# Two attentions in one kernel: how row maxima, row sums and outputs change their layout on the way between partitions and columns

## The chip, the cores and the metric

The program runs on one core of one Trainium2 chip. The metric is the device time of one execution in microseconds (us), the median of several. The core has TensorE (PE, matrix products into PSUM), VectorE (DVE), ScalarE (ACT), GpSimd (POOL, which here works on SBUF tiles alone) and SyncE (SP, which issues DMAs).

## The reference, cut to what matters

Four layers run one after the other on `x` (4 batches, 512 rows, 256 columns), with a context of 1601 rows per batch. Each of the two attentions has 8 heads, so 32 head passes.

```python
x = x + L0_xattn(ctx, layernorm(x))       # stage A: 8 heads of 128, keys: 512 + 1601 rows
x = x + L0_ffn(layernorm(x))              # stage B: top 2 of 8 experts
x = x + L1_xattn(ctx, layernorm(x))       # stage C: 8 heads of 32, keys: 1601 rows
x = x + L1_ffn(layernorm(x))              # stage D: top 2 of 8 experts
# in both attentions, for each batch and head:
attn = softmax(scale * q @ k.T)           # 512 x J, J = 2113 or 1601
out = attn @ v                            # 512 x 128, or 512 x 32
```

## The kernel before

Float32 precision is kept by splitting operands into a high and a low float16 half and making three products (`triple`), or, in stage C, by stacking the halves along the contraction.

**A head is a row of units.** In `attention0` a head `n` has 17 tiles of up to 128 keys, taken in pairs: 9 units, the last with one tile of 65 rows. In `attention1` there are 13 tiles in 7 units. In a unit TensorE makes the scores of its two tiles, transposed (keys on partitions, 512 queries along the columns), into one of two PSUM tiles `psS`; ScalarE takes the exponential twice, as float32 (`pf`) and as float16 (`ph`); VectorE or GpSimd makes the low half (`pl`); and TensorE multiplies both halves with the values into `psO`, some units later (`LAG`: 2 in stage A, 4 in stage C).

**Items.** Between these, at written-out places (`head_items`: unit, place 0 to 3), TensorE works on items, most of them for the next head, each in one of three PSUM tiles `psA` taken in turn. An item may start when the item three before it has been read. Items are: Q, K, V (projections), M (a block of 128 queries by 512 keys of plain scores, from which VectorE takes a row maximum), L (the same for the last few keys), X (the maxima, turned), S (the sums, turned, stage A), O (the output product, stage A), F (the output, turned, stage C), T, N (transposes), W (weights).

**The maximum.** Softmax needs, for each query, a number near the row's maximum. M and L give it with queries on partitions (`mc`, 128 by 4 float32). The scores have queries along columns, so item X turns `mc` into a row of 512 by four float32 transposes at TensorE. In stage A ScalarE then copies the negated row as bfloat16 into row 0 of `mrow` (the other 127 rows are zero), and each score tile gets a fourth product, `oneb` (ones) by `mrow`, that subtracts the maximum. In stage C VectorE writes the negated row as one more row of the stacked queries `qst`, which the score product contracts along with the rest.

**The sum.** In stage A GpSimd adds all 17 tiles of `pf` into `acc` (float32, 128 by 512, line L396). Item S (L613) multiplies `acc` with a column of fours, four float32 products of 128 by 128 with one column, and VectorE takes the reciprocal. In stage C the sum is a column of ones in the values.

**The output.** In stage C `psO` holds 65 rows: 32 of the high half of the values, 32 of the low half, one sum. VectorE copies them to `of` (`out_copy`). Item F multiplies four blocks of `of` with a constant matrix `fold` (65 by 33, float32) that adds the two halves and turns them; VectorE takes a reciprocal and multiplies.

Every engine works through its own list, written out in the same order (`for n`, `for u`, places), and waits on counting semaphores: `s_pG` for GpSimd's low halves, `s_fr` for what VectorE has read, `s_ah` for ScalarE, `s_acc` for the sums.

## Time and profile before

| | |
|---|---|
| time, median of 3 runs | 2724.38 us (2721.0 to 2725.88) |
| the profiled execution: time | 2723.15 us |
| its span | 2721.6 us |
| TensorE busy | 2477.8 us, 91% |
| VectorE busy | 1865.4 us, 69% |
| ScalarE busy | 1675.5 us, 62% |
| GpSimd busy | 1636.6 us, 60% |
| mean granted TensorE clock | 0.958 |

The span is the time from the first to the last instruction. Stage A's loop over heads lies from about 87 to 1505 us, stage B to 1820 us, stage C to 2377 us, stage D to the end. Busy time of TensorE counts a matmul from its start to its modelled end, and matmuls overlap: what one costs a full TensorE is the distance from its start to the next one's start.

### The profile page before, as it was taken

Reading aid. Unit: us, or ns where it says so; the run is one execution under the profiler, and the core shown is the slowest. Engines: PE = TensorE matmul, PEld = TensorE weight load, DVE = VectorE, ACT = ScalarE, POOL = GpSimd, SP = SyncE. Lnnn points to the kernel's source line nnn. Section 1 sums busy time; section 2 is a strip of 40 time slices with the busy share of each in tenths; the row PEclk is TensorE's granted clock in tenths of the full one; section 3 lists DMA queues with packets and bytes.
Section 4 is the critical chain, followed back from the end, with each engine's and each line's share of the span. In section 5 each row is a group of like instructions: output and inputs, shape, how many; then the busy total and the mean of one; then the engine's idle time right before and its main releaser. Section 6 shows DMA issues by size and latency. Waiting matters only on the chain. (4 is left out here: it accounts for less than half of the span.)

```text
span 2721.6 us, 46305 instructions
## 1 busy us (share of the span) xinstructions
PE 2477.8 (91%) x15187; PEld 1489.6 (55%) x15314; DVE 1865.4 (69%) x3467; ACT 1675.5 (62%) x2694; POOL 1636.6 (60%) x1442
## 2 busy tenths in 40 slices
PE   4999999999999999999999389867999999869997
PEld 2455555555555555555554268734555554447886
DVE  5678767787777786777676565347787888677443
ACT  3465665556655566555555375436787878758664
POOL 3467766677667676656567244416676769825443
PEclk9999999999999999999999589979999999969999
DMA  3000000000000000000000383231111101076223
GB/s 117 25 1 1 4 22 1 1 1 1 25 1 1 1 1 1 1 1 1 1 1 0 112 243 78 41 101 40 32 41 26 48 19 30 3 215 188 46 46 66
DMA packets 88377, 107.92 MB, mean 40 GB/s; under 512 B 16322, under 2 KB 77715, under 8 KB 88163
## 3 DMA queue, kind: packets, MB, share of 16 engines
q1 hardware_dynamic: 67140, 76.37, 9.3%
q0 software_dynamic: 19200, 24.97, 5.7%
q10 hardware_dynamic: 1856, 4.19, 0.4%
q8 instruction: 109, 1.79, 0.3%
q14 instruction: 72, 0.59, 0.1%
HBM read 68.75 MB, written 25.88 MB: 35 GB/s over the span
## 5 line engine op out<-in xcount | busy, mean ns | idle before, releaser
L396 POOL TENSOR_TENSOR a_acc<-a_acc,a_pf 128x512 f32<-128x512 f32 (+1 forms) x480 | 645.3, 1344 | 388.0 <-ACT a_pf L524 367.8
L1993 POOL TENSOR_TENSOR c_pl<-c_pf,c_ph 128x512 f16<-128x512 f32 x320 | 378.3, 1210 | 169.0 <-ACT c_ph L2092 168.7
L524 ACT ACTIVATE a_pf<-a_psS 128x1024 f32<-128x1024 f32 (+1 forms) x288 | 281.2, 976 | 303.8 <-PE a_psS L663 300.2
L813 DVE TENSOR_TENSOR a_pl<-a_pf,a_ph 128x512 f16<-128x512 f32 x448 | 405.4, 914 | 28.2 <-ACT a_ph L530 28.2
L789 DVE TENSOR_REDUCE a_mx<-a_psA 128x1 f32<-128x512 f32 x512 | 344.9, 685 | 48.8 <-PE a_psA L600 42.6
L530 ACT ACTIVATE a_ph<-a_psS 128x1024 f16<-128x1024 f32 (+1 forms) x288 | 281.0, 976 | 0.0
L1303 POOL DMA_INDIRECT f_sums<-f_xn,f_sidx x78 | 138.9, 1781 | 228.1 <-DVE f_xn L1668 191.6
L2324 DVE TENSOR_REDUCE c_mx<-c_psA 128x1 f32<-128x512 f32 x384 | 251.0, 685 | 34.4 <-PE c_psA L2163 32.4
L2085 ACT ACTIVATE c_pf<-c_psS 128x1024 f32<-128x1024 f32 x192 | 197.7, 1030 | 89.4 <-PE c_psS L2197 88.5
L784 DVE TENSOR_TENSOR a_vl<-a_psA,a_vh 128x256 f16<-128x256 f32 (+1 forms) x272 | 115.2, 423 | 167.2 <-ACT a_vh L469 164.3
L1162 DVE TENSOR_TENSOR f_xn<-f_xn 128x256 f16<-128x256 f32 x312 | 129.6, 424 | 127.8 <-ACT f_xn L1133 123.5
L685 PE MATMUL a_psO<-a_pl,a_vh 128*128 128x512 f16 (+1 forms) x544 | 206.8, 380 | 5.4 <-POOL a_pl L401 5.4
L679 PE MATMUL a_psO<-a_ph,a_vh 128*128 128x512 f16 (+1 forms) x544 | 207.1, 381 | 1.0 <-DVE a_ol L818 1.0
L542 PE MATMUL a_psS<-a_qh,a_kh 128*128 128x512 f16 (+1 forms) x544 | 206.2, 379 | 0.9 <-ACT a_mrow L485 0.8
L680 PE MATMUL a_psO<-a_ph,a_vl 128*128 128x512 f16 (+1 forms) x544 | 206.8, 380 | 0.0
L544 PE MATMUL a_psS<-a_qh,a_kl 128*128 128x512 f16 (+1 forms) x544 | 206.7, 380 | 0.0
L543 PE MATMUL a_psS<-a_ql,a_kh 128*128 128x512 f16 (+1 forms) x544 | 206.5, 380 | 0.0
L600 PE MATMUL a_psA<-a_kh,a_qh 128*128 128x512 f16 x512 | 194.3, 380 | 4.6 <-DVE a_kl L778 1.2
L778 DVE SCALAR_TENSOR_TENSOR a_kl<-a_psA,a_bkv,a_kh 128x512 f16<-128x512 f32 (+1 forms) x160 | 105.4, 659 | 134.3 <-ACT a_kh L463 134.3
L2092 ACT ACTIVATE c_ph<-c_psS 128x1024 f16<-128x1024 f32 x192 | 197.4, 1028 | 0.0
L1062 PE MATMUL f_psH<-f_xh,f_w 128*128 128x256 f16 x624 | 173.1, 277 | 17.7 <-ACT f_xn L1133 9.0
L463 ACT ACTIVATE a_kh<-a_psA,a_bkv 128x512 f16<-128x512 f32 (+1 forms) x160 | 98.3, 614 | 123.8 <-PE a_psA L544 123.8
(329 smaller groups left out, 6382.8 us busy)
## 6 DMA issues: line engine op xcount, KB each, us to landing
f_stage<-in_L_ffn_w SPq DMA_DIRECT2D x16, 1024.0 KB, 5.6
f_stage<-in_L_ffn_W SPq DMA_DIRECT2D x16, 1024.0 KB, 5.3
c_kst<-c_khs SPq DMA_DIRECT2D x64, 100.1 KB, 2.2
a_cx<-in_ctx SPq DMA_DIRECT2D x4, 1536.0 KB
c_cx<-in_ctx SPq DMA_DIRECT2D x12, 512.0 KB, 4.1
f_xrow<-f_xn SPq DMA_DIRECT2D x8, 512.0 KB, 3.2
f_sums<-X SPq DMA_DIRECT2D x2, 2048.0 KB, 12.4
c_kst<-c_kls SPq DMA_DIRECT2D x32, 100.1 KB, 2.2
```

The source lines that it names most:

```text
L396: g.tensor_tensor(acc[0:k, p, :], acc[0:k, p, :], pf[0:k, q % RF, i, :], ALU.add).then_inc(s_acc, 1)
L524: act.activation(pf[0:r, q % RF, 0:k, :], psS[q % 2][0:r, 0:k, :], ACT.Exp, scale=SCALE).then_inc(s_pF, 1)
L530: act.activation(ph[0:r, q % RP, 0:k, :], psS[q % 2][0:r, 0:k, :], ACT.Exp, scale=SCALE).then_inc(s_pH, 1)
L543: pe.matmul(out, hi, xl_, start=False, stop=False)
L544: return pe.matmul(out, lo, xh_, start=False, stop=last)
L679: pe.matmul(psO[:, :], vh[0:r, g % 2, j, vs], ph[0:r, q % RP, i, :], start=(j == 0), stop=False)
L680: pe.matmul(psO[:, :], vl[0:r, g % 2, j, vs], ph[0:r, q % RP, i, :], start=False, stop=False)
L685: ins = pe.matmul(psO[:, :], vh[0:r, g % 2, j, vs], pl[0:r, q % RP, i, :], start=False, stop=(j == JT0 - 1))
L789: v.tensor_reduce(mx[:, n % 2, it, c:c + 1], ps[:, 0:KCH[c][1]], AX.X, ALU.max).then_inc(s_fr, 1)
L813: v.tensor_tensor(pl[0:r, q % RP, i, :], pf[0:r, q % RF, i, :], ph[0:r, q % RP, i, :], ALU.subtract).then_inc(s_pL, 1)
L1993: g.tensor_tensor(pl[0:r, q % RP, i, :], pf[0:r, q % RF, i, :], ph[0:r, q % RP, i, :], ALU.subtract).then_inc(s_pG, 1)
L2324: ins = v.tensor_reduce(mx[:, n % 2, it, c:c + 1], ps[:, 0:KCH[c][1]], AX.X, ALU.max)
```

## The change

1. **Stage A, maxima.** Item X and ScalarE's copy go. GpSimd multiplies a negated identity with the maxima, broadcast (`row`): `mrow` then holds, in each block of 128 columns, a diagonal matrix with the negated maxima, and the product with ones sums its columns. `row(n + 1)` stands in the last but one unit (`TOP`), ahead of that unit's sums. TensorE waits for it ahead of the fourth product of a head's first score tile.
2. **Stage A, sums.** ScalarE copies `acc` to float16 (`sum_hi`, at the head of unit 1 of the next head), GpSimd makes the low half (`sum_lo`, at the head of unit 2), and item S makes eight float16 products.
3. **Stage C, maxima.** `mc` is float16, and item X multiplies with a float16 identity.
4. **Stage C, outputs.** Item F is four plain transposes of `of` (65 rows), without `fold`; VectorE adds the two halves in PSUM, with one instruction more.

```diff
@@ stage A
-                               (6, 3, ("L", m)), (7, 2, ("X", m))):
+                               (6, 3, ("L", m))):
...
+            def sum_lo(n):
+                g.wait_ge(s_sh, n + 1)
+                if n >= 1:
+                    g.wait_ge(s_it, IDX[("S", n - 1)] + 1)
+                g.tensor_tensor(sl[:, :], acc[:, n % 2, :], sh[:, :], ALU.subtract).then_inc(s_sl, 1)
+
+            def row(n):
+
+                g.wait_ge(s_mc, n + 1)
+                g.tensor_tensor(mrow[:, n % 2, :].rearrange("p (t q) -> p t q", q=P),
+                                minus[:, :].unsqueeze(1).broadcast_to([P, ST, P]),
+                                mc[:, n % 2, :].unsqueeze(2).broadcast_to([P, ST, P]), ALU.mult).then_inc(s_mrow, 1)
...
+                    if n >= 1 and u == SUM_AT:
+                        sum_lo(n - 1)
+                    if u == TOP and n + 1 < NH:
+                        row(n + 1)
                     sums(n, u)
...
-                elif what[0] == "X":
-                    act.wait_ge(s_it, i + 1)
-                    act.activation(mrow[0:1, what[1] % 2, :], ps[0:1, :], ACT.Copy, scale=-1.0).then_inc(s_ah, 1)
...
+            def sum_hi(n):
+                act.wait_ge(s_acc, added(uid(n, U - 1)))
+                if n >= 1:
+                    act.wait_ge(s_it, IDX[("S", n - 1)] + 1)
+                act.activation(sh[:, :], acc[:, n % 2, :], ACT.Copy).then_inc(s_sh, 1)
...
+                    if n >= 1 and u == SUM_AT - 1:
+                        sum_hi(n - 1)
...
-                    pe.wait_ge(s_acc, added(uid(n, U - 1)))
+                    pe.wait_ge(s_sl, n + 1)
                     for it in range(ST):
-                        ins = pe.matmul(ps[:, it:it + 1], acc[:, n % 2, it * P:(it + 1) * P], four[:, :], start=True,
-                                        stop=True)
-                elif what[0] == "X":
-                    n = what[1]
-                    pe.wait_ge(s_mc, n + 1)
-                    for it in range(ST):
-                        ins = pe.transpose(ps[0:1, it * P:(it + 1) * P], mc[:, n % 2, it:it + 1], identf[:, :])
+                        for part in (sh, sl):
+                            ins = pe.matmul(ps[:, it:it + 1], part[:, it * P:(it + 1) * P], four[:, :],
+                                            start=part is sh, stop=part is sl)
...
-                        pe.wait_ge(s_ah, after_act(("X", n)))
                 ps = psS[q % 2][0:r, i, :]
                 triple(ps, kh[:, p, js], kl[:, p, js], qh[:, p, :], ql[:, p, :], True, False)
+                if u == 0 and i == 0:
+                    pe.wait_ge(s_mrow, n + 1)
@@ stage C
-                        ins = pe.transpose(ps[0:1, it * P:(it + 1) * P], mc[:, n % 2, it:it + 1], identf[:, :])
+                        ins = pe.matmul(ps[0:1, it * P:(it + 1) * P], mc[:, n % 2, it:it + 1], ident[:, :], start=True,
+                                        stop=True)
...
-                        ins = pe.matmul(ps[:, it * (DH + 1):(it + 1) * (DH + 1)], of[:, it * P:(it + 1) * P],
-                                        fold[:, :], start=True, stop=True)
+                        ins = pe.transpose(ps[:, it * VC:(it + 1) * VC], of[:, it * P:(it + 1) * P], identf[0:VC, 0:VC])
...
+                    v.reciprocal(rl[:, n % 2, :], pt[:, :, 2 * DH]).then_inc(s_rl, 1)
+                    v.tensor_reduce(both, pt[:, :, 0:2 * DH].rearrange("p t (a n) -> p t n a", a=2), AX.X, ALU.add).then_inc(s_rl, 1)
+                    v.wait_ge(s_rl, 2 * n + 2)
```

The change moves work between engines at three places. GpSimd, stage A, from a head's last low half for unit 4 to the next head's unit 2. Before (`a_pl` is a low half, `a_acc` the sum, `X` the output rows):

```order
L401 TENSOR_TENSOR a_pl<-a_pf,a_ph 128x512
L396 TENSOR_TENSOR a_acc<-a_acc,a_pf 128x512 x2
L362 TENSOR_TENSOR X<-X,a_yt 128x256 x2
L401 TENSOR_TENSOR a_pl<-a_pf,a_ph 128x512
L396 TENSOR_TENSOR a_acc<-a_acc,a_pf 128x512 x2
```

Now:

```order
L421 TENSOR_TENSOR a_pl<-a_pf,a_ph 128x512
L414 TENSOR_TENSOR a_mrow<-a_minus,a_mc 128x512
L403 TENSOR_TENSOR a_acc<-a_acc,a_pf 128x512 x2
L403 TENSOR_TENSOR a_acc<-a_acc,a_pf 65x512
L398 TENSOR_TENSOR a_acc<-a_pf 128x512
L403 TENSOR_TENSOR a_acc<-a_acc,a_pf 128x512 x2
L409 TENSOR_TENSOR a_sl<-a_acc,a_sh 128x512
L403 TENSOR_TENSOR a_acc<-a_acc,a_pf 128x512 x6
```

Two instructions of 512 columns are new per head: the diagonal right behind the head's last low half (that of unit 6), the low half of the sum behind the next head's unit 1.

TensorE, stage C, around item F, before:

```order
L2163 MATMUL c_psA<-c_kst,c_qst 128x512
L2180 MATMUL c_psA<-c_fold,c_of 128x33 x4
L2221 MATMUL c_psO<-c_ph,c_vst 65x512
L2226 MATMUL c_psO<-c_pl,c_vst 65x512
L2197 MATMUL c_psS<-c_qst,c_kst 128x512
L2169 MATMUL c_psA<-c_kst,c_qst 128x65 x4
```

Now:

```order
L2188 MATMUL c_psA<-c_kst,c_qst 128x512
L2206 MATMUL c_psA<-identf,c_of 128x65 x4
L2246 MATMUL c_psO<-c_ph,c_vst 65x512
L2251 MATMUL c_psO<-c_pl,c_vst 65x512
L2222 MATMUL c_psS<-c_qst,c_kst 128x512
L2194 MATMUL c_psA<-c_kst,c_qst 128x65 x4
L2222 MATMUL c_psS<-c_qst,c_kst 128x512
L2246 MATMUL c_psO<-c_ph,c_vst 65x512
L2251 MATMUL c_psO<-c_pl,c_vst 65x512
L2246 MATMUL c_psO<-c_ph,c_vst 65x512
L2251 MATMUL c_psO<-c_pl,c_vst 65x512
L2200 MATMUL c_psA<-c_ident,c_mc 1x128 x4
```

The order is as it was; F (L2180, now L2206) gives 65 columns instead of 33, and X (now L2200) takes another identity.

VectorE, stage C, the same place, now:

```order
L2349 TENSOR_REDUCE c_mx<-c_psA 128x1 x2
L2362 RECIPROCAL c_rl<-c_psA 128x4
L2363 TENSOR_REDUCE c_psA<-c_psA 128x128
L2367 TENSOR_TENSOR c_yt<-c_psA,c_rl 128x128
L2352 TENSOR_REDUCE c_mx<-c_psA 128x4
L2306 TENSOR_REDUCE c_mc<-c_mx 128x4
L2378 TENSOR_TENSOR c_pl<-c_pf,c_ph 128x512
L2356 TENSOR_SCALAR c_qst<-c_psA 1x512
```

One row is new, L2363, the sum of the two halves. It stands between item F and the maxima that item X turns.

## Rows read from the trace of the kernel before

**Rows 1.** The page: span, busy times, granted clock in 40 slices

```profile
span 2721.6 us, 46305 instructions
PE 2477.8 (91%) x15187; PEld 1489.6 (55%) x15314; DVE 1865.4 (69%) x3467; ACT 1675.5 (62%) x2694; POOL 1636.6 (60%) x1442
PEclk9999999999999999999999589979999999969999
```

**Rows 2.** Windows of stages A and C: length, busy PE PEld DVE ACT POOL, clock, DMA

```profile
87.00:1505.00 1418.00, 1399.72 (x7806) 758.83 (x7930) 1027.04 (x1700) 847.95 (x1265) 963.43 (x792) 1.00 0.01 3
1820.00:2377.00 557.00, 511.69 (x2660) 272.00 (x2660) 436.51 (x751) 419.38 (x488) 396.54 (x358) 0.95 0.13 32
```

**Rows 3.** Waits of TensorE in stage A: us, times, longest

```profile
PE a_psO L685 <- POOL a_pl L401: 5.4, 6, 2.0
```

**Rows 4.** Timeline of TensorE, stage A: start, us, line

```profile
612.42 0.29 PE L607 MATMUL a_psA<-a_kh,a_qh 128*128 128x65 f16 x4
612.54 0.38 PE L542 MATMUL a_psS<-a_qh,a_kh 128*128 128x512 f16 x1
822.24 0.38 PE L600 MATMUL a_psA<-a_kh,a_qh 128*128 128x512 f16 x1
822.45 0.95 PE L613 MATMUL a_psA<-a_four,a_acc 128*128 128x1 f32 x8
823.26 0.38 PE L679 MATMUL a_psO<-a_ph,a_vh 128*128 128x512 f16 x1
842.40 0.60 PE L619 MATMUL a_psA<-identf,a_mc 128*1 128x128 f32 x4
842.84 0.38 PE L679 MATMUL a_psO<-a_ph,a_vh 128*128 128x512 f16 x1
```

**Rows 5.** Timeline of GpSimd, stage A, a usual head and one with more work

```profile
841.98 1.15 POOL L401 TENSOR_TENSOR a_pl<-a_pf,a_ph 128x512 f16<-128x512 f32 x1
843.09 4.61 POOL L396 TENSOR_TENSOR a_acc<-a_acc,a_pf 128x512 f32<-128x512 f32 x3
258.51 1.15 POOL L401 TENSOR_TENSOR a_pl<-a_pf,a_ph 128x512 f16<-128x512 f32 x1
```

**Rows 6.** Timeline of TensorE and ScalarE at the same two places

```profile
844.78 0.38 PE L685 MATMUL a_psO<-a_pl,a_vh 128*128 128x512 f16 x1
259.81 0.38 PE L685 MATMUL a_psO<-a_pl,a_vh 128*128 128x512 f16 x1 [0.40 <-POOL a_pl L401]
848.46 0.38 PE L663 MATMUL a_psS<-a_mrow,a_oneb 128*128 128x512 bf16 x1
854.28 0.69 ACT L463 ACTIVATE a_kh<-a_psA,a_bkv 128x512 f16<-128x512 f32 x1 [2.23 <-PE a_psA L544]
```

**Rows 7.** Timeline of TensorE, stage C, one head and a chunk's transposes

```profile
2068.14 0.28 PE L2122 MATMUL c_psA<-identf,c_cx 65*128 65x65 f32 x2
2310.22 0.38 PE L2221 MATMUL c_psO<-c_ph,c_vst 128*65 128x512 f16 x1 [0.81 <-DVE c_of L2357]
2310.87 0.98 PE L2180 MATMUL c_psA<-c_fold,c_of 65*128 65x33 f32 x8
2311.68 0.38 PE L2221 MATMUL c_psO<-c_ph,c_vst 128*65 128x512 f16 x1
2313.54 0.60 PE L2175 MATMUL c_psA<-identf,c_mc 128*1 128x128 f32 x4
2313.98 0.38 PE L2197 MATMUL c_psS<-c_qst,c_kst 97*65 97x512 f16 x1
```

**Rows 8.** Timeline of VectorE, stage C, in the same head

```profile
2311.07 0.69 DVE L2324 TENSOR_REDUCE c_mx<-c_psA 128x1 f32<-128x512 f32 x1 [0.40 <-PE c_psA L2163]
2311.88 0.18 DVE L2335 RECIPROCAL c_rl<-c_psA 128x4 f32<-128x4 f32 x1
2312.66 0.43 DVE L2327 TENSOR_REDUCE c_mx<-c_psA 128x4 f32<-128x260 f32 x1 [0.27 <-PE c_psA L2169]
2313.12 0.17 DVE L2281 TENSOR_REDUCE c_mc<-c_mx 128x4 f32<-128x16 f32 x1
```

More of the change, by code:

```diff
@@ L95, in attention0 @@
     TOP = U - 2
+    SUM_AT = 2
     ON_POOL = {(4, 1), (5, 1), (6, 1)}
@@ L150, in opening @@
         out.insert(out.index(("M", 0, 0, 0)), ("B", 0))
-        return out + [("L", 0), ("B", 1), ("V", 0, v), ("X", 0)]
+        return out + [("L", 0), ("B", 1), ("V", 0, v)]
     OPEN = opening()
@@ L261, in attention0 @@
         oneb = sb("oneb", [P, P], BF16)
+        minus = sb("minus", [P, P], BF16)
         onef = sb("onef", [P, P], F32)
-        four = sb("four", [P, 1], F32)
+        four = sb("four", [P, 1], F16)
         zcol = sb("zcol", [P, 1], F32)
@@ L299, in attention0 @@
         s_mc = sem("mc")
+        s_mrow = sem("mrow")
         s_sP = sem("sP")
@@ L306, in attention0 @@
         s_acc = sem("acc")
+        s_sh = sem("sh")
+        s_sl = sem("sl")
         s_oH = sem("oH")
@@ L343, in _ @@
         def _(g):
-            for t, v in ((mhalf, -0.5), (onef, 1.0), (four, 4.0), (mv, 0.0), (oneb, 1.0), (mrow, 0.0), (zcol, 0.0)):
+            for t, v in ((mhalf, -0.5), (onef, 1.0), (four, 4.0), (mv, 0.0), (oneb, 1.0), (zcol, 0.0)):
                 g.memset(t[:], v).then_inc(s_const, 1)
+            g.tensor_scalar(minus[:, :], identf[:, :], -1.0, None, ALU.mult).then_inc(s_const, 1)
             g.wait_ge(s_const, 7)
@@ L407, in _ @@
                 item(what)
+            row(0)
             g.wait_ge(s_fr, after_dve(("B", 1)))
@@ L425, in _ @@
                             item(what)
+            sum_lo(NH - 1)
             for what in CLOSE:
@@ L533, in _ @@
                         item(what)
+            sum_hi(NH - 1)
             out_hi(NH - 1)
@@ L1871, in attention1 @@
         cth, ctl = sb("cth", [P, 2, KC, 512], F16), sb("ctl", [P, 2, KC, 512], F16)
-        mx, mc = sb("mx", [P, 2, ST, NK]), sb("mc", [P, 2, ST])
+        mx, mc = sb("mx", [P, 2, ST, NK]), sb("mc", [P, 2, ST], F16)
+        ident = sb("ident", [P, P], F16)
         pf = sb("pf", [P, RF, 2, S])
@@ L1916, in attention1 @@
         names = ("L1_xattn_Wq", "L1_xattn_Wk", "L1_xattn_Wv")
-        NCONST = 7
+        NCONST = 5
         @block.sync
@@ L1973, in rstds @@
                 g.tensor_scalar(ve[:, :], mv[:, :, 1], EPS, None, ALU.add).then_inc(s_pool, 1)
-                g.wait_ge(s_pool, b + 1 if b == 0 else 2 + b + 1)
+                g.wait_ge(s_pool, b + 1 if b == 0 else b + 2)
                 g.tensor_tensor(rstd[:, :], ve[:, :], mhalf[:, :], ALU.pow).then_inc(s_rstd, 1)
-            for i, (t, val) in enumerate(((mhalf[:, :], -0.5), (ones, 1.0), (fold[:, :], 0.0), (fold[2 * DH:VC, DH:DH + 1], 1.0),
+            for i, (t, val) in enumerate(((mhalf[:, :], -0.5), (ones, 1.0),
                                           (vst[:, :, :, :, 2 * DH:VC], WS), (vf[:, :, :, DH:2 * DH], 0.0),
@@ L1982, in _ @@
             rstds(0)
-            g.wait_ge(s_rstd, 1)
-            for i in range(2):
-                g.affine_select(out=fold[0:2 * DH, 0:DH], in_=fold[0:2 * DH, 0:DH], compare_op=ALU.not_equal, fill=1.0,
-                                base=-i * DH, pattern=[[-1, DH]], channel_multiplier=1).then_inc(s_pool, 1)
-                g.wait_ge(s_pool, i + 2)
+            g.tensor_copy(ident[:, :], identf[:, :]).then_inc(s_pool, 1)
             def low(q, i):
@@ L2233, in _ @@
             pe.wait_ge(s_const, NCONST)
-            pe.wait_ge(s_pool, 3)
+            pe.wait_ge(s_pool, 2)
             for what in FIRST:
@@ L2333, in item @@
                     n = what[1]
-                    pt = ps[:, 0:ST * (DH + 1)].rearrange("p (t n) -> p t n", n=DH + 1)
-                    v.reciprocal(rl[:, n % 2, :], pt[:, :, DH]).then_inc(s_rl, 1)
-                    v.wait_ge(s_rl, n + 1)
+                    pt = ps[:, 0:ST * VC].rearrange("p (t n) -> p t n", n=VC)
+                    both = ps[:, ST * VC:ST * VC + ST * DH].rearrange("p (t n) -> p t n", n=DH)
+                    v.reciprocal(rl[:, n % 2, :], pt[:, :, 2 * DH]).then_inc(s_rl, 1)
+                    v.tensor_reduce(both, pt[:, :, 0:2 * DH].rearrange("p t (a n) -> p t n a", a=2), AX.X, ALU.add).then_inc(s_rl, 1)
+                    v.wait_ge(s_rl, 2 * n + 2)
                     if n >= 2:
                         v.wait_ge(s_x, n - 1)
-                    ins = v.tensor_tensor(yt[:, n % 2, :, :], pt[:, :, 0:DH],
+                    ins = v.tensor_tensor(yt[:, n % 2, :, :], both,
                                           rl[:, n % 2, :].unsqueeze(2).broadcast_to([P, ST, DH]), ALU.mult)
```

10 lines of the change are left out of this document (5 added, 5 removed).

## The prediction

> **What bounds the kernel now.** I read the windows of the two stages first, then who TensorE waits for, then the timeline at the places that the change touches. The page gives the span of the profiled execution, 2721.6 us, with TensorE busy for 91% of it and at full clock in nearly all of stage A [rows 1]. In stage A TensorE is busy 1399.7 of 1418 us [rows 2]: it is the bound, and what shortens its list shortens the stage, as long as no other engine takes over. The others stand at 60 to 72% there; GpSimd, which gets work from the change, at 963 of 1418 us. Its low halves already make TensorE wait, but only 5.4 us in 6 waits [rows 3]. In stage C TensorE is busy 511.7 of 557 us, the others 71 to 78% [rows 2]; here the slack is less clear, and I follow one head.
>
> What a matmul costs a full TensorE is the distance from start to start, not its duration: 512 float16 columns take 0.21 to 0.22 us (822.24 to 822.45), though the row says 0.38 [rows 4].
>
> **Stage A, the sums (S).** Four float32 products of 128 by 128 with one column are eight records, and they hold TensorE from 822.45 to 823.26, 0.81 us, 0.10 each [rows 4]. They become eight float16 products with one column. The nearest row is item L: four products of 65 float16 columns, each with its own 128 by 128 weights, in 0.12 us (612.42 to 612.54), 0.03 each [rows 4]. A shorter one can't cost more than that unless its weight load is the limit, and these four had such loads. I take 8 x 0.03 = 0.24 us, so 0.57 saved per head. Bounds: 0.2 for the eight below, 0.81 (no gain) above.
>
> A rule of the Trainium skill speaks against this. TensorE: Matmul & The Clock Gate, section LDWEIGHTS, has a weight load take columns / 1.2 ns, which is 107 ns for 128 columns whatever the type, an estimate of 0.85 us for eight and so nothing gained. The trace's float32 records at 0.10 us agree with it, its float16 ones at 0.03 don't, and the sum goes by these.
>
> **Stage A, the maxima (X).** Four float32 transposes hold TensorE from 842.40 to 842.84, 0.44 us [rows 4]. They go, and the product with `mrow` keeps its shape, so its 0.22 us stay. 0.44 saved per head, and ScalarE's copy with it, whose place `sum_hi` takes.
>
> **Who hides the new work.** GpSimd gets two instructions of 512 columns per head. Its low halves of that size take 1.15 us, its sums up to 4.61 / 3 = 1.5 [rows 5]; I take 1.2 each, 1.5 as the upper bound for the one with two broadcast inputs, which no row shows. That is 77 us more, 1040 of a stage of some 1390: 75%. What counts is where they stand.
> - The diagonal stands behind the head's last low half, which ends at 841.98 + 1.15 = 843.13, so it is done at 844.4. TensorE needs it for the first product with `mrow` of the next head, at 848.46 [rows 5, 6]. 4 us of slack.
> - The last low half itself is needed at 844.78 [rows 6], 1.65 us after it is done. GpSimd's run that leads to it starts with an exponential of unit 4, behind S but ahead of X. So the gain at S moves both, and the gain at X comes out of the 1.65 us: it fits, in a usual head. In the three heads that also add the output bias, TensorE waits 0.40 for it already (259.81) [rows 6]; there X's 0.44 turn into wait. The other three of the six waits lie in the last two heads, whose TensorE has less to do; there too I count nothing.
> - In those three heads the low half ends at 258.51 + 1.15 = 259.66 [rows 5] and the diagonal at 260.9 (261.2 at 1.5). TensorE wants it seven products after 259.81, at 261.3. It just fits.
> - The sum of the head is complete at 843.09 + 4.61 = 847.70 now and at 848.9 then [rows 5]. ScalarE's copy of it stands ahead of the K item at 854.28, before which ScalarE was idle for 2.23 us, from 852.05 [rows 6]. Behind the copy are queued that K item and the exponential of unit 1, for which TensorE's next scores wait; 3.2 us of slack hide it. The low half (1.2) comes behind the sums of unit 1, and S reads it in unit 3. Without that cover each would cost its full wait.
>
> At the end of the stage nothing hides the copy and the low half of the last sum: some 0.6 + 1.2 us between the sum and S in place of none, in part beside the last output's own path, and the last head is short for GpSimd. I take +1.5. At the opening, TensorE no longer stops for a turned row ahead of the first scores: -0.7, from the 0.44 and a copy, against the 1.2 of GpSimd that three products hide in part. Stage A: -(30 x 0.57) - (27 x 0.44) + 1.5 - 0.7 = -28.2 us.
>
> **Stage C.** X: four products of 128 float16 columns lie between the 0.03 of 65 and the 0.22 of 512 [rows 4], so 0.055 each, 0.22 in place of 0.44 (2313.54 to 2313.98) [rows 7]: 0.22 saved. F: eight records from 2310.87 to 2311.68, 0.81 us [rows 7], become four transposes of 65 columns. Two such, float32 from 65 rows, last 0.28 together, of which one alone is about 0.2 (0.29 less three steps of 0.03 in L's row [rows 4]): a step of at most 0.08. Half of a 128-column transpose's 0.11 is 0.055. I take 0.25 for four, 0.56 saved; the upper bound is the 0.10 of the float32 records now, 0.41 for four and 0.40 saved. Together 0.78 per head.
>
> But VectorE pays. The new sum of halves reads 256 elements from PSUM, and a reduction of 260 takes 0.43 us [rows 8]. It stands between F and the maxima that X waits for. Followed through: F would be done at 2311.12, but VectorE is in the reduction that began at 2311.07, so its reciprocal begins at about 2311.7 (now 2311.88). With 0.1, 0.43 and some 0.25 for the product the reduction of L starts at 2312.5 (now 2312.66, where it waits for TensorE), the maxima are there 0.6 later, as now, at 2313.15 [rows 8], and X starts at 2313.2. TensorE would be ready for it at 2313.54 - 0.56 = 2312.98. So X waits 0.2 us, and F's 0.56 shrink to 0.34. With X's 0.22 the head gains 0.56.
>
> The wait for `of` stays: TensorE stands 0.81 us at 2310.22 in each such head [rows 7], for a copy that follows a reduction that follows TensorE's own product. All that moves together. Heads with items for the next batch have more of TensorE's work between F and X, and may gain the full 0.78; I take 0.56 for all, and 31 heads, since the first one of the stage ends in a wait for a load. Stage C: -17.4 us.
>
> **Sum.** -28.2 - 17.4 = -45.6. The profiled execution took 2723.15 us, so 2677.6; the median of the runs lay 1.2 above it, hence 2678.
>
> **The rivals.** (a) VectorE takes more of stage C: if the sum of halves costs 0.6 to 0.8 us, for its strided input or for the wait for two results, F's gain is gone, and stage C gives 31 x 0.22 = 7 us. For it speaks VectorE's 78% and the single reduction's worth of room; against it, that the row of 260 elements is of the same kind. 2688.
> (b) S costs what it did, by the weight loads: 30 x 0.57 come back, 2695. Against it are the four loads in 0.12 us.
> (c) GpSimd takes over in the late units of stage A: TensorE's 5.4 us of waits grow by X's gain, 12 us; 2690. For it speaks that it works without a break there (841.98 to 847.70), against it the 1.65 us.
> (d) Slower than before: ScalarE, a strict list, stands before the copy of the sum and holds the exponentials behind it. That begins once GpSimd completes the sum more than 3.2 us later than now, and costs 32 us for each further us; from 3.2 + 45.6 / 32 = 4.6 us on the kernel is slower than before. It would take a diagonal product of over 4 us, three times what any row of that size takes. At 5.5 us later: 2678 + 32 x 2.3 = 2752.
>
> **How the numbers follow.** Forecast 0.74 (its own range 2664 to 2688: below, the full 0.78 in stage C and 0.2 us for S, 57 us in all; above, F at its upper bound and the diagonal late in some heads), (a) 0.10, (b) 0.05, (c) 0.06, (d) 0.04, no effect at all 0.01. Range 2662 to 2694, which leaves out (d), most of (b) and the edges. Faster means by over 0.2%, below 2719, about what a measurement of this kernel tells from no change: 0.94. Same 0.02, slower 0.04.
>
> **What the profile after would show.** S in about 0.24 us (wrong: near 0.8, that is (b)); no X and no new wait of a score product for GpSimd in stage A; heads shorter by 1.0 us there; at most 0.9 us of wait for a low half in the bias heads; F in 0.25 us; a wait of X for the maxima of about 0.2 us in heads without items for the next batch, and those heads 0.56 us shorter. Wrong would make it: a sum of halves well above 0.43 us, ScalarE waiting for GpSimd's sum in each head, or a diagonal product of several us.

## The result and the profile after

The changed kernel took 2696.76 us (median of 4 runs, 2693.58 to 2698.33), the kernel before 2724.02 us (median of 4 on the same chip, 2721.0 to 2725.88). The ratio is 0.9899, with a 95% interval of 0.9882 to 0.9917: faster by some 27 us. The prediction had 2678 and a range up to 2694. The sign and most of the steps were right; 19 us of the forecast gain of 46 are missing, and the time is outside the range.

The page of the kernel after; its rows answer to [rows 1]:

```profile
span 2695.6 us, 46041 instructions
PE 2436.9 (90%) x15057; PEld 1425.6 (53%) x15058; DVE 1903.7 (71%) x3499; ACT 1675.4 (62%) x2694; POOL 1734.4 (64%) x1503
```

The windows of stages A and C after, with the columns of [rows 2]:

```profile
85.00:1492.00 1407.00, 1377.47 (x7807) 724.70 (x7806) 1056.25 (x1700) 850.42 (x1266) 1059.67 (x858) 0.99 0.01 3
1800.00:2349.00 549.00, 495.11 (x2550) 243.12 (x2550) 445.40 (x786) 420.83 (x490) 399.74 (x357) 0.95 0.13 34
```

TensorE's busy time fell by 22 us in stage A and by 17 in stage C. But stage A's window is only 11 us shorter: of the 22 us taken out, some half came back as idle time. VectorE runs the same 1700 instructions there as before and is busy for 29 us *more* (1056 against 1027). An engine whose work has not grown and whose busy time has is being slowed, and this is the line to follow up.

The waits of TensorE in stage A after, with the columns of [rows 3]:

```profile
PE a_psO L714 <- POOL a_pl L421: 15.6, 7, 3.2
PE a_psA L574 <- DVE a_kl L807: 5.0, 7, 0.9
PE a_psO L708 <- DVE a_ol L847: 3.9, 4, 1.8
```

GpSimd's low half makes TensorE wait 15.6 us instead of 5.4, and the longest of these waits is 3.2 us. Of the waits in the two last rows there was one each before (0.9 us for `a_kl`, 1.0 for `a_ol`); now there are 7 and 4.

To place the time I measured from one head's reciprocal of the sums to the next one's (of `a_rl` in stage A, of `c_rl` in stage C), in both traces. The first of them comes 2.3 us earlier, the 31 heads that follow in stage A take 10.9 us less, those of stage C 15.7 us less, and what lies between the stages and behind stage C takes 1.4 us more each time. The sum is 26.0, the difference of the spans. Head by head in stage A, where head n is what ends with the n-th reciprocal after the first (us, from the trace):

| heads | before | after | forecast |
|---|---|---|---|
| 4 to 7, 12 to 15, 20 to 29 | e.g. 43.73 | 42.73 | -1.01 |
| 8, 16 | 43.73 | 43.82 | -1.01 |
| 1, 9, 17 | 44.39 | 43.64 | -1.01 |
| 2, 10, 18 | 45.00 | 44.54 | -1.01 |
| 3, 11 (with the bias) | 45.81 | 49.44 | -0.57 |
| 19 (with the bias) | 45.80 | 47.75 | -0.57 |

Eighteen heads did what was forecast, to 0.01 us. Three gave back 10.9 us against the forecast, eight more 4.6. The last two, which the forecast had 1.5 us longer for the end of the stage, became 1.6 longer together, and the opening with its one head gained 2.3 for a forecast of 1.7.

**Head 3.** GpSimd's timeline in the kernel after (start, us, line):

```profile
252.27 2.77 POOL L369 TENSOR_TENSOR X<-X,a_bb 128x256 f32<-128x256 f32 x4
255.00 3.54 POOL L421 TENSOR_TENSOR a_pl<-a_pf,a_ph 128x512 f16<-128x512 f32 x1
258.50 1.08 POOL L414 TENSOR_TENSOR a_mrow<-a_minus,a_mc 128x512 bf16<-128x512 bf16 x1
```

VectorE's timeline at the same place, after:

```profile
254.96 1.05 DVE L782 TENSOR_SCALAR a_cx<-a_cx,a_mv,a_rstd 128x256 f32<-128x256 f32 x3
255.92 1.28 DVE L842 TENSOR_TENSOR a_pl<-a_pf,a_ph 128x512 f16<-128x512 f32 x2
257.13 1.56 DVE L782 TENSOR_SCALAR a_cx<-a_cx,a_mv,a_rstd 128x256 f32<-128x256 f32 x2
```

And VectorE's there in the kernel before, where GpSimd's low half began at 258.51 and took 1.15 [rows 5]:

```profile
258.90 2.18 DVE L753 TENSOR_SCALAR a_cx<-a_cx,a_mv,a_rstd 128x256 f32<-128x256 f32 x2
```

Both engines read and write SBUF here, and the rows look as if one of them stood still while the other works. Before, GpSimd began 0.39 us ahead of VectorE; its low half took 1.15 and VectorE's two norms 2.18, where three alone take 1.05. After, VectorE began 0.04 us ahead; four norms (0.40 each) and two low halves (0.68 each) ran at full speed one behind the other, and GpSimd's low half took 3.54. It ended at 258.54; less its own 1.15, it got nowhere until about 257.4, when VectorE had a last norm to make, of 65 rows. That one took 1.24. TensorE and its clock behind it, after (a timeline, then a window of five us, whose last three values are clock, DMA share and GB/s):

```profile
258.69 0.40 PE L714 MATMUL a_psO<-a_pl,a_vh 128*128 128x512 f16 x1 [3.23 <-POOL a_pl L421]
259.31 0.63 PE L709 MATMUL a_psO<-a_ph,a_vl 128*128 128x512 f16 x1
259.00:264.00 5.00, 5.00 (x17) 1.90 (x16) 1.13 (x1) 0.40 (x1) 4.78 (x4) 0.67 0.01 2
```

TensorE waits 3.23 us where it waited 0.40 [rows 6], and just after the standstill it starts eight products at the lower of its two clock levels, 1.2 GHz: they stand 0.43 apart, not 0.22, some 1.7 us more. 2.83 + 1.7 is 4.5 of the 4.6 us that the head is above the trend of its neighbours. In head 19 the wait is the same 3.23 and the clock stays up; it lost 3.0.

The Trainium skill, SBUF — State Buffer, section Who interferes with whom, says that VectorE and GpSimd share a pair of ports, that the instruction which starts first has it to the end, and that the other one blocks fully. It says so for VectorE instructions with two inputs in SBUF, as the low halves have, and for those in a mode that uses two ports, which a `tensor_scalar` such as the norms can enter; no run here shows in which mode the norms ran. On who waits for whom, these two traces agree with it. The page speaks of one instruction; here the low half of 1.15 us stayed out over four norms and two low halves, 2.4 us, and why it was let in only then no run shows.

**The new waits for VectorE.** TensorE in head 8, after, at the first product of the V item, and VectorE ahead of it:

```profile
503.85 0.28 PE L574 MATMUL a_psA<-a_wkvh,a_xth 128*128 128x256 f16 x1 [0.66 <-DVE a_kl L807]
501.83 1.29 DVE L842 TENSOR_TENSOR a_pl<-a_pf,a_ph 128x512 f16<-128x512 f32 x1
503.05 0.74 DVE L807 SCALAR_TENSOR_TENSOR a_kl<-a_psA,a_bkv,a_kh 128x512 f16<-128x512 f32 x1
```

V's product takes the PSUM buffer that `a_kl` still reads. It used to come 0.57 us later, behind the long float32 S. And the low half ahead of `a_kl` takes 1.29 us beside GpSimd, where it takes 0.68 alone and took 0.68 before. V stands 0.82 us later for it; with the M item at 498.92, which starts 0.26 late behind `a_vl`, that is what head 8 lies above the forecast. The 448 low halves of VectorE in stage A are busy for 440.9 us after and for 405.4 before. Of these 35 us not all are the change's: in `stage_c_only` below, whose stage A is that of the kernel before, they are busy for 419.7, with every head but the last as long as before. VectorE's busy time pointed to the right place, but what it costs has to be read from TensorE's waits.

**Stage C.** TensorE in a head without items for the next batch, after (F at L2206, X at L2200):

```profile
2285.22 0.41 PE L2206 MATMUL c_psA<-identf,c_of 65*128 65x65 f32 x4
2285.46 0.38 PE L2246 MATMUL c_psO<-c_ph,c_vst 128*65 128x512 f16 x1
...
2287.10 0.38 PE L2251 MATMUL c_psO<-c_pl,c_vst 128*65 128x512 f16 x1
2287.53 0.38 PE L2200 MATMUL c_psA<-c_ident,c_mc 128*1 128x128 f16 x4
2287.84 0.41 PE L2222 MATMUL c_psS<-c_qst,c_kst 97*65 97x512 f16 x1
...
2288.73 0.38 PE L2251 MATMUL c_psO<-c_pl,c_vst 128*65 128x512 f16 x1
2289.19 0.38 PE L2222 MATMUL c_psS<-c_qst,c_kst 97*128 97x512 f16 x1
```

And VectorE beside it:

```profile
2286.02 0.17 DVE L2362 RECIPROCAL c_rl<-c_psA 128x4 f32<-128x4 f32 x1
2286.11 0.40 DVE L2363 TENSOR_REDUCE c_psA<-c_psA 128x128 f32<-128x256 f32 x1
2286.76 0.42 DVE L2352 TENSOR_REDUCE c_mx<-c_psA 128x4 f32<-128x260 f32 x1
2287.21 0.17 DVE L2306 TENSOR_REDUCE c_mc<-c_mx 128x4 f16<-128x16 f32 x1
2287.30 1.03 DVE L2378 TENSOR_TENSOR c_pl<-c_pf,c_ph 128x512 f16<-128x512 f32 x1
2288.35 0.69 DVE L2356 TENSOR_SCALAR c_qst<-c_psA 1x512 f16<-1x512 f32 x1
```

F takes 0.24 us (0.25 forecast), the sum of halves 0.40 (0.43). X starts 0.43 behind the product ahead of it, 0.21 more than one step; the forecast had 0.2 of waiting there, but `f_later` below shows that only 0.12 of it is a wait. X's four float16 products start 0.055 apart, as forecast (their row's 0.38 is three steps and one product of 0.22), and yet the next score starts 0.31 behind the first of them, not 0.22: it comes 0.15 behind the last. And 0.24 us are lost once more ahead of the next head's first score, which needs VectorE's write of the row (L2356). That write comes late behind a low half that now takes 1.03 us; here too VectorE works beside GpSimd. Such a head went from 13.86 to 13.63, not by 0.56 but by 0.23. Heads with items for the next batch gained more than forecast: 21.65 to 20.44, 21.97 to 19.74. Part of the latter is scatter: the same head takes 20.89 us in `maxima_only` and 21.04 in `small_delay`, whose stage C is that of the kernel before, and from stage C's first to its last reciprocal these two take 505.0 and 505.3 us, not 507.1. So stage C's 15.7 us hold to about 2.

### The profile page after: what moved, and what is told of

It is laid out like the page before. It is cut to its first block and busy times, and to the rows that moved or that the text cites. A ratio compares the mean times of both kernels' runs of the same rounds, so it can differ in the third digit from the quotient of the medians.

```text
span 2695.6 us, 46041 instructions
## 1 busy us (share of the span) xinstructions
PE 2436.9 (90%) x15057; PEld 1425.6 (53%) x15058; DVE 1903.7 (71%) x3499; ACT 1675.4 (62%) x2694; POOL 1734.4 (64%) x1503
## 5 line engine op out<-in xcount | busy, mean ns | idle before, releaser
L842 DVE TENSOR_TENSOR a_pl<-a_pf,a_ph 128x512 f16<-128x512 f32 x448 | 440.9, 994 | 23.9 <-ACT a_ph L561 23.7
L714 PE MATMUL a_psO<-a_pl,a_vh 128*128 128x512 f16 (+1 forms) x544 | 207.1, 381 | 15.6 <-POOL a_pl L421 15.6
L692 PE MATMUL a_psS<-a_mrow,a_oneb 128*128 128x512 bf16 (+1 forms) x544 | 206.9, 380 | 1.5 <-POOL a_mrow L414 1.5
```

What stands on the lines that cost most here:

```text
L714: ins = pe.matmul(psO[:, :], vh[0:r, g % 2, j, vs], pl[0:r, q % RP, i, :], start=False, stop=(j == JT0 - 1))
L842: v.tensor_tensor(pl[0:r, q % RP, i, :], pf[0:r, q % RF, i, :], ph[0:r, q % RP, i, :], ALU.subtract).then_inc(s_pL, 1)
```

## Experiments

Each ratio is against the kernel before on the same chip.

**The change in parts.** The first three kernels are the kernel before with one part: the sum in float16 halves (`sum_hi`, `sum_lo`, S with `four` in float16); the maxima of stage A on diagonals (`row`, no X, none of the sums' halves); stage C alone.

```
sums_only:    + g.tensor_tensor(sl, acc[n % 2], sh, ALU.subtract)      X kept
maxima_only:  - (7, 2, ("X", m))    + g.tensor_tensor(mrow, minus, mc, ALU.mult)      S kept in float32
stage_c_only: - mc = sb("mc", [P, 2, ST])     + mc = sb("mc", [P, 2, ST], F16)     F by transposes
```

> Stage A's sums in float16 halves alone, all else as before. Contention theory (GpSimd's low half for unit 6 of the head that adds the bias stretched from 1.15 to 3.54 us because VectorE's instructions on SBUF tiles ran back to back beside it, and the shift of phase brought them there): the product saves 0.6 us in each of 30 heads, and the total depends on whether this shift alone brings them together: 17 us faster if not, about 8 us faster if so, with the long low half visible. Work theory (GpSimd simply has too much to do late in a head once both of its new instructions are there): no long low half here, 17 us faster.

Measured: 2712.01 us against 2718.61, ratio 0.9972 (0.9963 to 0.9982). That is 6.6 us, short of both theories' 17, and near the 8 without the long low half that was to explain it. Heads without other trouble are 0.57 shorter (43.74 to 43.17): S's term is right. No low half took 3.54 and the bias heads stayed at 45.81. But heads 8 and 16 are 0.52 *longer* than before, and the waits for `a_kl` are there, 5.0 us in 7. Heads 1, 2, 8 to 10 and 16 to 18 together are 4.6 us above their forecast, as much as with the whole change: all of that loss comes with the sums.

> Stage A's maxima on diagonals alone, all else as before. Contention theory: 0.44 us saved in 27 heads, 12 us faster, less 3 x 2.8 us if VectorE's instructions fall beside the low half. Work theory: the diagonal product is the second instruction in the late units, so some wait of TensorE for the low half in unit 8 appears in heads that have none now, and the gain is 5 us or less.

Measured: 2713.83 against 2718.61, ratio 0.9983 (0.9973 to 0.9992), 4.8 us. Ordinary heads are 0.44 shorter, as forecast for X, heads 1, 2, 8 to 10 and 16 to 18 among them, and none waits for a low half as the work theory has it. Heads 3, 11 and 19 took 49.43, 47.76 and 47.75, and in each a low half took 3.54 us. So the long low half comes with X's removal and not with the copy or the halves of the sum.

> Stage C's part of the change alone (float16 product for the maxima, plain transposes and a sum of halves for the output). As the trace after has it: 15 to 16 us faster, nearly all within stage C. If stages A and C disturbed each other (clock, phase of loads), another number than the 15.7 us that stage C gained between its first and last output.

Measured: 2705.23 against 2718.61, ratio 0.9948 (0.9931 to 0.9964), with stage C 15.8 us shorter from the first to the last reciprocal. The timed gain is 13.4 us (10 to 19), a little under the expected 15 to 16. Within the 2 us of scatter, stage C's share is its own and doesn't depend on stage A. The three parts gained 6.6, 4.8 and 13.4 us, 24.8 in all, against some 27 for the whole change.

**The bias heads: what kept the low half out?** Two kernels, each the changed kernel with one entry of a table moved. The first moves VectorE's norms out of the place, the second GpSimd's addition of the bias, so that the low half comes 2.7 us earlier.

```
norms_moved:  - (3, 7): [("cn", 8, 11)], (3, 8): [("cn", 11, 13)], (4, 0): [("sn", 0, 4)]}
              + (4, 1): [("cn", 8, 11)], (4, 2): [("cn", 11, 13)], (4, 3): [("sn", 0, 4)]}
bias_moved:   - BIAS_AT = (3, 7)
              + BIAS_AT = (4, 1)
```

> The changed kernel, with VectorE's last five normalizations of the context (units 7 and 8 of head 3) moved to units 1 and 2 of head 4; GpSimd's work is untouched. Contention theory: the low half of unit 6 in that head takes 1.2 to 1.6 us again instead of 3.54, TensorE's wait there falls from 3.2 to about 0.9 us, and with it the fall of the clock: 7 to 10 us faster than the changed kernel, near 2688. Work theory: GpSimd is as late as before, no change, 2697.

Measured: 2692.38 against 2718.61, ratio 0.9900 (0.9883 to 0.9916), no better than the change. The trace says why; GpSimd, VectorE and TensorE of `norms_moved` in head 3:

```profile
255.08 2.24 POOL L421 TENSOR_TENSOR a_pl<-a_pf,a_ph 128x512 f16<-128x512 f32 x1
255.03 2.84 DVE L842 TENSOR_TENSOR a_pl<-a_pf,a_ph 128x512 f16<-128x512 f32 x3
257.46 0.38 PE L714 MATMUL a_psO<-a_pl,a_vh 128*128 128x512 f16 x1 [1.93 <-POOL a_pl L421]
```

VectorE's own low halves moved up into the gap, started 0.05 us ahead and kept GpSimd's out as the norms had, for 1.1 us (in head 11 it got in behind the first of them, and took 1.65); the rest of the gain went into new waits of 0.6 to 0.7 us where the norms now stand. So it isn't the norms as such: a run of low halves on VectorE does it too. My expectation of 7 to 10 us missed that.

> The changed kernel, with GpSimd's four adds of the next batch's output bias moved from unit 7 of head 3 to unit 1 of head 4, where it is idle. The low half of unit 6 then starts 2.8 us earlier, while VectorE works on PSUM or stands still. Contention theory: it takes 1.15 us in all three heads, TensorE's 3.2 us of wait go, heads 3, 11 and 19 shrink from 47.7 to 49.4 us to about 44.8: 12 us faster than the changed kernel, a ratio of 0.9855 to the kernel before. Rival, that a long low half is GpSimd's own (an instruction fetch, say): it stays at 3.5 us, but is done in time, so that the time falls as well; the row tells them apart.

Measured: 2685.22 against 2724.21, ratio 0.9858 (0.9841 to 0.9874), as expected. GpSimd and VectorE of `bias_moved` in head 3:

```profile
252.37 1.15 POOL L421 TENSOR_TENSOR a_pl<-a_pf,a_ph 128x512 f16<-128x512 f32 x1
254.49 4.01 POOL L403 TENSOR_TENSOR a_acc<-a_acc,a_pf 128x512 f32<-128x512 f32 x3
255.06 3.59 DVE L782 TENSOR_SCALAR a_cx<-a_cx,a_mv,a_rstd 128x256 f32<-128x256 f32 x3
```

The low half is done before VectorE's run begins and takes its 1.15. The norms now meet GpSimd's sums, which started first, and take 3.59 in place of 1.05, until the sums end; nobody waits for them. Heads 3, 11 and 19 take 44.80, 1.01 less than before, and stage A ends 12.1 us earlier than with the change. The collision is still there; it has only moved to where it costs nothing.

**Is the order of two starts enough?** The kernel *before*, with a fill of 0.52 us on GpSimd ahead of the low half in the three bias heads: nothing of the change, only the phase.

```
+                    if b + 1 < B and (h, u) == BIAS_AT:
+                        g.memset(dummy[:, :], 0.0)
```

> The kernel before, untouched but for one GpSimd instruction of about 0.5 us (a fill of a tile that nobody reads), ahead of the low half of unit 6 in heads 3, 11 and 19. There the low half started at 258.51 and VectorE's run on SBUF tiles at 258.90, so 0.5 us turns their order round. Contention theory (whoever starts first keeps the other waiting): the low half takes about 3.5 us instead of 1.15, TensorE waits 0.4 + 0.5 + 2.4 = 3.3 us there instead of 0.4: about 9 us slower than before, 11 with a fall of the clock, ratio 1.003 to 1.004. Work theory: the 0.5 us alone, 3 x 0.5 = 1.5 us slower.

Measured: 2724.59 against 2723.70, ratio 1.0003 (0.9994 to 1.0013), where 1.003 to 1.004 was expected. VectorE now started first in all three heads, but GpSimd's low half was kept out in one alone. VectorE and GpSimd of `small_delay` in head 3 and in head 19, with TensorE's wait in the latter:

```profile
258.24 2.84 DVE L756 TENSOR_SCALAR a_cx<-a_cx,a_mv,a_rstd 128x256 f32<-128x256 f32 x3
258.31 1.34 POOL L402 TENSOR_TENSOR a_pl<-a_pf,a_ph 128x512 f16<-128x512 f32 x1
...
977.38 1.05 DVE L756 TENSOR_SCALAR a_cx<-a_cx,a_mv,a_rstd 128x256 f32<-128x256 f32 x3
977.45 3.51 POOL L402 TENSOR_TENSOR a_pl<-a_pf,a_ph 128x512 f16<-128x512 f32 x1
981.11 0.38 PE L688 MATMUL a_psO<-a_pl,a_vh 128*128 128x512 f16 x1 [3.23 <-POOL a_pl L402]
```

The starts are the same to a hundredth of a us, 0.07 apart, and yet in head 3 VectorE pays (2.84 for norms of 1.05; low half 1.34), since GpSimd gets in behind its first norm, and in head 19 GpSimd does (3.51), at 4.08 us for the head. Head 11 went like head 3. A stretched low half thus needs nothing of the change, and the answer to the question is no: the order of the two starts, as the rows have it, doesn't settle by itself who pays. In the changed kernel a lead of 0.04 to 0.05 us was enough for VectorE in three heads of three, and here 0.07 was enough in one. The median of the runs didn't move, so the single profiled execution (span 2730.9) doesn't say how often the tie goes that way. How often it does in the changed kernel I can't say either, but `bias_moved` shows that its median carries the loss.

**The waits for `a_kl`.** S one place later, behind the V item, so that V stands where it stood:

```
-            at[3][2].append(("S", n - 1))
+            at[3][3].append(("S", n - 1))
```

> The changed kernel with item S one place later in unit 3, behind the V item instead of ahead of it. If the 0.66 us waits of a V item for VectorE's low half of the keys come only from S having become 0.6 us shorter ahead of it, they go with S behind it (7 heads), and the time falls by 3 to 5 us. If VectorE is late for another reason (contention with the low half of the sum), they stay.

Measured: 2691.71 against 2724.21, ratio 0.988 (0.9863 to 0.9896). Heads 8 and 16 take 43.18 instead of 43.82; the last reciprocal of stage A comes 4.2 us earlier than with the change. The six V waits are gone, and S waits 1.6 us in all for the same `a_kl`. The time is within what was expected, but both readings hold in part: `a_kl` is still late, and S meets it with a shorter wait.

**Stage C: X's price.** The kernel before with X alone as float16 products:

```
- ins = pe.transpose(ps[0:1, it * P:(it + 1) * P], mc[:, n % 2, it:it + 1], identf[:, :])
+ ins = pe.matmul(ps[0:1, it * P:(it + 1) * P], mc[:, n % 2, it:it + 1], ident[:, :], start=True, stop=True)
```

> Of stage C's part only the float16 product for the maxima; the output still by the constant matrix. The changed kernel's trace has this item at 0.31 us against 0.44 before: 0.12 us x 31 = 4 us faster than the kernel before, and no wait for the maxima. If all of stage C's gain came from here, 13 us.

Measured: 2724.25 against 2724.21, ratio 0.9997 (0.9988 to 1.0007): nothing, where 4 us were expected. (`mc` is float16 here too.) TensorE of `c_maxima_only`, and the loads of X's weights, which have an engine name of their own, PEld:

```profile
2299.95 0.38 PE L2229 MATMUL c_psO<-c_pl,c_vst 128*65 128x512 f16 x1
2300.25 0.38 PE L2177 MATMUL c_psA<-c_ident,c_mc 128*1 128x128 f16 x4
2300.57 0.41 PE L2200 MATMUL c_psS<-c_qst,c_kst 97*65 97x512 f16 x1
2300.81 0.38 PE L2224 MATMUL c_psO<-c_ph,c_vst 128*65 128x512 f16 x1
2300.25 0.20 PEld L2177 LDWEIGHTS c_psA<-c_ident,c_mc 128*1 128x1 f16 x4 [0.41 <-issue]
```

From the value product ahead of X to the value product behind the score there are 0.86 us. In the kernel before, the same piece has this first and last row, and these loads for X:

```profile
2299.46 0.38 PE L2226 MATMUL c_psO<-c_pl,c_vst 128*65 128x512 f16 x1
2300.33 0.38 PE L2221 MATMUL c_psO<-c_ph,c_vst 128*65 128x512 f16 x1
2299.54 0.44 PEld L2175 LDWEIGHTS c_psA<-identf,c_mc 128*1 128x1 f32 x4 [0.19 <-issue]
```

That is 0.87. Among themselves the four products are as cheap as forecast: they start 0.055 apart where the transposes stood 0.11 apart. The 0.22 are lost where TensorE changes over: X starts 0.30 to 0.31 after the product ahead of it instead of 0.22, the score starts 0.15 after X's last product instead of one more step of 0.055, and the product behind the score 0.24 after it instead of 0.22. It is so in all 32 heads. The first load of X's weights starts with the product (2300.25), where the transposes' starts 0.14 ahead of them (2299.54, they at 2299.68). That fits the late start; what holds it back no run shows. The term of 0.22 us per head was 0.01.

**Stage C: the chain through VectorE.** F in the last unit, behind X, so that its reciprocal and sum of halves don't stand ahead of the maxima:

```
-            at[LAG][2].append(("F", n - 1))
+            at[TOP][1].append(("F", n - 1))
```

> The changed kernel with item F of stage C moved from unit 4, ahead of the maxima's way, to unit 6, behind it. If the sum of halves on VectorE is what holds back the maxima (0.2 us) and the row (0.24 us), both waits go: 0.45 us in at least 14 heads and up to 31, 6 to 14 us faster than the changed kernel. If a new wait takes their place (the next head's first maxima behind F's 1.0 us on VectorE), less than 3 us.

Measured: 2686.74 against 2724.21, ratio 0.9864 (0.9845 to 0.9883). Heads without items for the next batch take 13.32 us (after: 13.63), 0.54 less than before. TensorE of `f_later`:

```profile
2266.85 0.38 PE L2251 MATMUL c_psO<-c_pl,c_vst 128*65 128x512 f16 x1
2267.16 0.39 PE L2200 MATMUL c_psA<-c_ident,c_mc 128*1 128x128 f16 x4
2267.47 0.41 PE L2222 MATMUL c_psS<-c_qst,c_kst 97*65 97x512 f16 x1
...
2268.61 0.38 PE L2251 MATMUL c_psO<-c_pl,c_vst 128*65 128x512 f16 x1
2268.83 0.38 PE L2222 MATMUL c_psS<-c_qst,c_kst 97*128 97x512 f16 x1
```

X starts 0.31 behind its predecessor, as it does without any wait in `c_maxima_only`, not 0.43: so its wait for the maxima in the changed kernel was 0.12 us. The wait ahead of the next head's score is gone. With F out of VectorE's way, F's 0.56 arrive nearly in full. The gain over the changed kernel is 9.5 us by the ratios, within the 6 to 14 expected. Of the 12.5 us that stage C gains between its first and last reciprocal (491.4 to 478.9), 2.5 are only that F itself stands elsewhere: the first reciprocal comes that much later.

**Together.** `combined` is the changed kernel with the edits of `bias_moved`, `s_later` and `f_later`.

> The changed kernel with all three moves: the bias adds in unit 1 of head 4, item S behind V, item F in unit 6. If they are independent, their gains add: 12 + 4 + 10 = 26 us below the changed kernel, ratio to the kernel before 0.9805. If they share a bound, less than 20.

Measured: 2674.13 against 2723.70, ratio 0.982 (0.9803 to 0.9836). By the ratios that is 21.5 us below the changed kernel, where 26 were expected and the three measured alone give 25.9 together; the interval just takes that in. In the traces the stages add up: stage A from its first to its last reciprocal is 16.3 us shorter (12.2 and 3.7 with `bias_moved` and `s_later` alone), stage C 12.3 (12.5 with `f_later`). Between the two lie 2.3 us more than in `f_later`, in places that the edits don't touch.

`sum_low_later` is `combined` with `sum_lo` behind the sums of unit 2 instead of ahead of them, against the waits for `a_ol`:

```
-                    if n >= 1 and u == SUM_AT:
-                        sum_lo(n - 1)
                     ...
                     sums(n, u)
+                    if n >= 1 and u == SUM_AT:
+                        sum_lo(n - 1)
```

> The combined kernel with GpSimd's low half of the sum behind the sums of unit 2 instead of ahead of them. In heads 2, 10 and 18 VectorE's three normalizations took 2.69 us beside it (1.04 alone) and TensorE waited 0.71 us for the output's low half. Contention theory: that wait goes, about 2 us faster than combined. If the low half of the sum then comes late for item S, a wait for it shows in every head and it is slower.

Measured: 2675.47 against 2723.70, ratio 0.9818 (0.9801 to 0.9834), no difference. The waits of 0.71 us for `a_ol` are gone, heads 8 and 16 come down to 42.69, but heads 2, 10 and 18 are 1.05 longer and heads 3 and 19 1.6 and 1.4: GpSimd and VectorE meet elsewhere.

`last_head` is `combined` with the low halves of the last head all on VectorE and its sum turned by the old float32 products, since nothing hides a copy and a low half there:

```
+        return n < NH - 1 and (w, i) in ON_POOL
+                    if n == NH - 1:
+                        pe.matmul(ps[:, it:it + 1], acc[:, n % 2, it * P:(it + 1) * P], fourf[:, :], ...)
```

> The combined kernel, with stage A's last head as follows: all low halves on VectorE, which has no maxima to make there, and its sum turned by the float32 product, so that no copy and no low half stand at the end. The waits for GpSimd in the last head (0.9, 2.2, 1.2 and 1.5 us) should go: 4 to 6 us faster than combined.

Measured: 2670.72 against 2723.70, ratio 0.9804 (0.9788 to 0.9821), 3.4 us below `combined`, a little less than expected and within the noise of the two. The last head takes 23.45 us instead of 25.82: its waits for GpSimd's low halves are gone, but item S now waits 3.6 us for GpSimd's sum. It has the lowest time of all, some 53 us below the kernel before and 26 below the changed one.

## Why the prediction was wrong, step by step

**Right.** S: eight products 0.025 apart, 0.20 us in all; the forecast was 0.24. TensorE in a usual head after, the first rows of S and what follows it:

```profile
816.99 0.17 PE L646 MATMUL a_psA<-a_four,a_sh 128*128 128x1 f16 x1
817.01 0.16 PE L646 MATMUL a_psA<-a_four,a_sl 128*128 128x1 f16 x1
...
817.19 0.38 PE L708 MATMUL a_psO<-a_ph,a_vh 128*128 128x512 f16 x1
```

Rival (b) falls with it, and so does the 0.85 us that the prediction made of eight weight loads by TensorE: Matmul & The Clock Gate, section LDWEIGHTS, of the Trainium skill. The page's 107 ns are the length of one load, and the trace is near it: a load for S lasts 0.096 us. But the eight start 0.025 apart, so they overlap, and their lengths don't add up. Also right were X's 0.44 in stage A, F and the sum of halves. So was the cover of the new work. The diagonal product took 1.03 to 1.08 us in 28 of 32 heads, no score waited for it but the first of all (1.48 us at 83.86), and ScalarE waited for GpSimd's sums only in the last two heads, so (d) had nothing to stand on.

**The step that failed** is the one on the last low half in the bias heads: "there X's 0.44 turn into wait", at most 0.9 us. The step took GpSimd's low half for a thing of fixed length, 1.15 us, and moved it in time. It was 1.15 only because it began 0.39 us ahead of VectorE's norms. X's removal brought the V item, and the `a_vl` of VectorE behind it, 0.44 us forward (its wait for ScalarE's `a_vh` went from 1.70 to 1.26), but not GpSimd, whose run starts with an exponential ahead of X. 0.39 of lead against 0.44 of shift: the order flipped. This cost 10.9 us, of which the rows give 10.6: 8.5 of waiting beyond the 0.40 that was there (3 times 2.83) and 3.4 of lower clock in two heads, less the 1.3 that the forecast had already given up (3 times 0.44). `maxima_only` shows the trigger, `bias_moved` the cost in timed runs, `small_delay` that the low half can be kept out without anything of the change. That the flip of order is what does it rests on the rows: the low half was kept out in each of the twelve bias heads of the four traces in which VectorE led by 0.04 to 0.05 us, and took 1.15 us in each of the twelve of four traces in which GpSimd led by 0.38 to 0.39 (`before`, `sums_only`, `stage_c_only`, `c_maxima_only`); with a lead of 0.07 in `small_delay` VectorE won one of three. Rival (c) named the engine, and the sum of TensorE's waits for its low halves grew by 10.2 us, near the 12 of (c). But (c) put that on X's gain in the late units of all heads; the ordinary heads have no such wait.

**Not priced at all:** that V follows S and would meet `a_kl`, and that GpSimd's two new instructions slow VectorE. These are 4.6 us in heads 1, 2, 8 to 10 and 16 to 18. `sums_only` has all of them and `maxima_only` none, so of GpSimd's two instructions the diagonal costs nothing in these heads. `s_later` shows the first cause. The second is read from the rows (1.29 and 2.69 us for what alone takes 0.68 and 1.05) and was tested only by `sum_low_later`, which moved the meeting and gained nothing in sum; its share of the 4.6 isn't shown.

**Stage C** came out at -15.7 for -17.4, but by luck and not by its own sum: of the 31 heads fifteen gave 0.22 to 0.27, ten 0.36 to 0.6, and six gave 0.8 to 2.2, part of it scatter. The term "0.22 saved" for X was mis-sized: its step of 0.055 from product to product was right, but it took the change to these products and away from them for free, and with that the term is 0.01 (`c_maxima_only`). X's wait for the maxima was 0.12, not 0.2. And the step from F's 0.56 to 0.34 stopped at X, while the same chain went on to the write of the row, for another 0.24 us. F's 0.57 less 0.12 and 0.24, with X's 0.01, give the 0.22 that such a head gained.

**Rest.** The tail of stage A was put at +1.5, and the last two heads are 1.6 us longer together. The last S does wait 1.55 us for its low half (at 1490.36). But head 30 alone is 1.1 longer, and its wait for a low half of GpSimd and one for `a_ol` grew from 1.1 and 1.0 to 1.6 and 1.8; the forecast counted nothing there, so that the number came out is luck. Between the stages and behind stage C, 1.4 us each were added in places that the change doesn't touch. The two pieces took 366.2 and 347.0 us after; in other profiled runs they lie 1.5 to 2.7 us off (364.7 and 349.1 in `bias_moved`, 368.9 for the first in `small_delay`), so I take it for scatter, which isn't shown. Two sums of the prediction are off by themselves, without weight for the outcome: 2677.6 and 1.2 are 2678.8, not 2678, and the terms of its lower edge come to some 54 us, not 57.

-45.6 forecast, +10.9 and +4.6 in stage A's heads, -0.5 for its opening and its last heads together, +1.7 in stage C, +2.8 outside: -26.1, for 26.0 measured.

## What to carry to other kernels

When a change shifts TensorE's list, look up every place where GpSimd's instruction on the critical path and a run of VectorE instructions on SBUF start within the shift of each other: the durations in the trace hold for the present order of the starts only, and the price of the other order is the length of VectorE's run, not a few tenths. An item that is made shorter also brings its followers nearer to the buffers that they take; moving one entry behind its follower gave back here what the shortening had cost. Where a chain runs through a second engine, follow it to the last instruction queued there, since a late row can stop the next head after the first wait has been counted.

## What the hardware showed that I had not expected

- A low half of GpSimd that came 0.04 to 0.05 us behind the first of a run of VectorE instructions on SBUF took 3.54 us instead of 1.15, twelve times of twelve: it stayed out over four norms and two low halves. At 0.07 us between the starts it was let in behind the first norm in two heads of one execution, and stayed out in the third. The other way round, VectorE's 1.05 became 3.59.
- In all of these long rows, and in the 2.24 of `norms_moved`, GpSimd got in as VectorE turned to a block of 65 rows instead of 128; in the shorter ones, of 1.34 and 1.65, it got in between two blocks of 128. No run here varies the rows.
- Four products with one column of float16 weights and 128 moving columns start 0.055 us apart, half of the 0.11 of the float32 transposes of the same data, and save nothing: with the change to them and away from them the piece takes 0.86 us instead of 0.87. Eight products with 128 columns of weights and one moving column start 0.025 apart, and the change to and from them costs nothing that the rows show.
- Four float32 transposes from 65 rows with 65 columns take 0.24 us, about half of what four with 128 columns take.
- After 3.2 us without work TensorE ran some eight products at 1.2 GHz in two heads of the changed kernel, and none in a third with the same wait. Over all traces its clock fell behind nine of thirteen such waits.
